# A transformer block on one core: where the reciprocals, the softmax sums and the input load stand in their slots

## The reference

```
x = x + layernorm(attention(layernorm(x)))
x = x + layernorm(ffn(layernorm(x)))

attention:  q, k, v = x @ w_q, x @ w_k, x @ w_v          # 16 heads of 64
            q = l2norm(q) * exp(scale);  k = l2norm(k)
            out = softmax(q @ k.T) @ v  ->  out @ w_out + b_out
ffn:        h = silu(x @ w1 * s1) * (x @ w2 * s2)        # 1024 wide
            h = gelu(h @ h1 * t1);  h = gelu(h @ h2 * t2);  h @ w3 * s3
```

## Time and profile before

| | us |
|---|---|
| median of 3 runs | 1771.52 (1770.67 to 1775.65) |
| the profiled execution | 1771.27 |
| its span, first to last instruction | 1769.4 |
| TensorE busy in the span | 1703.3 (96%) |
| VectorE busy | 1184.2 (67%) |
| ScalarE busy | 1010.7 (57%) |
| GpSimd busy | 461.4 (26%) |

### The profile page before, as it was taken

How to read it: one execution, slowest core, us unless ns; L and a number is a source line. 1 busy time by engine, 2 the same in 40 slices (tenths; PEclk the granted TensorE clock), 3 DMA queues, 4 the chain that set the end, 5 groups by cost and what they waited for, 6 DMA issues and landing times.

```text
span 1769.4 us, 24647 instructions
## 1 busy us (share of the span) xinstructions
PE 1703.3 (96%) x8584; PEld 1421.9 (80%) x8584; DVE 1184.2 (67%) x2033; ACT 1010.7 (57%) x1349; POOL 461.4 (26%) x557
## 2 busy tenths in 40 slices
PE   5999999999999999999999987999999999999998
PEld 4788888788888888888888775788888888888887
DVE  5777877877877877877877876635454545445454
ACT  4877778778778777777778765223223231323231
POOL 3533533533533533533633321000000000000000
PEclk9999999999999999999999999999999999999999
DMA  4545555456455456455455653300000000000000
GB/s 130 131 116 127 123 126 139 108 126 143 103 132 138 104 130 150 105 126 123 101 117 131 149 153 100 116 2 4 22 24 1 24 1 25 0 25 1 24 1 24
DMA packets 73473, 151.44 MB, mean 86 GB/s; under 512 B 27904, under 2 KB 28288, under 8 KB 73344
## 3 DMA queue, kind: packets, MB, share of 16 engines
q1 hardware_dynamic: 65712, 122.87, 29.2%
q10 hardware_dynamic: 6624, 23.21, 4.5%
q0 software_dynamic: 1008, 3.67, 0.5%
HBM read 56.91 MB, written 20.19 MB: 44 GB/s over the span
## 4 chain that ended last, share of the span: by engine, by line
PE 76%; DVE 8%; DMA 6%; issue 5%; ACT 3%; SPq 2%; POOL 1%; DVEq 0%; ACTq 0%; POOLq 0%
PE bank L1061 15%; PE pair L1139 13%; PE pair L1140 13%; PE bank L1003 10%; PE pair L1044 4%; PE pair L1045 4%; PE bank L1075 4%; PE pair L1130 3%; PE pair L1131 3%; DVE Pl L714 3%; PE bank L1030 2%; DMA Dp<-work 2%; PE bank L1168 2%; PE bank L1169 2%; DMA work<-rows 1%
## 5 line engine op out<-in xcount | busy, mean ns | idle before, releaser
L1139 PE MATMUL pair<-hh,f 128*128 128x512 f32 x1024 | 400.7, 391 | 2.6 <-DVE hl L832 2.2
L1140 PE MATMUL pair<-hl,f 128*128 128x512 f32 x1024 | 399.5, 390 | 0.0
L1061 PE MATMUL bank<-Ph,V 128*128 128x512 f32 x1024 | 367.3, 399 | 20.9 <-DVE Pl L714 19.1
L501 ACT ACTIVATE P<-pair,sh 128x1024 f32<-128x1024 f32 x256 | 286.3, 1118 | 159.8 <-PE pair L1045 136.3
L714 DVE TENSOR_TENSOR Pl<-P,Ph 128x1024 fp32r<-128x1024 f32 x256 | 315.4, 1232 | 0.3
L1003 PE MATMUL bank<-w,xh 128*128 128x256 f32 (+1 forms) x1024 | 285.3, 341 | 6.1 <-DVE turned L708 2.8
L549 ACT ACTIVATE hr<-pair,ct 128x512 f32<-128x512 f32 x128 | 88.3, 690 | 355.0 <-PE pair L1140 355.0
L506 ACT ACTIVATE Ph<-P 128x1024 fp32r<-128x1024 f32 x256 | 271.9, 1062 | 8.1
L1061 PEld LDWEIGHTS bank<-Ph,V 128*128 128x128 f32 x1024 | 192.9, 188 | 83.8 <-issue 38.9
L1139 PEld LDWEIGHTS pair<-hh,f 128*128 128x128 f32 x1024 | 192.8, 188 | 46.6 <-DVE hl L832 5.9
L1140 PEld LDWEIGHTS pair<-hl,f 128*128 128x128 f32 x1024 | 192.8, 188 | 39.9
(11 more groups left out here) (104 smaller groups left out, 2660.3 us busy)
## 6 DMA issues: line engine op xcount, KB each, us to landing
stack<-turned SPq DMA_DIRECT2D x128, 384.0 KB, 4.0
stack<-turned SPq DMA_DIRECT2D x128, 256.0 KB, 4.7
work<-rows SPq DMA_DIRECT2D x128, 128.0 KB, 2.9
f<-raw ACTq DMA_DIRECT2D x22, 512.0 KB, 4.9
raw<-in_h ACTq DMA_DIRECT2D x16, 512.0 KB, 4.0
xt<-in_x SPq DMA_DIRECT2D x8, 512.0 KB, 8.2
xr<-in_x SPq DMA_DIRECT2D x8, 512.0 KB, 4.6
x<-xr SPq DMA_DIRECT2D x8, 512.0 KB, 5.7
```

Of the source, the lines that this page charges most:

```text
L501: e.activation(M.P[:, i % 2, :], M.SB[i % 2][:, :], ACT.Exp, bias=M.sh[:, h:h + 1]).then_inc(S["exp"])
L1061: d = e.matmul(M.OB[:, :], v, p[:, u % 3, j * 512:(j + 1) * 512], start=jt == 0 and m == 0, stop=jt == 3 and m == 2)
L1139: e.matmul(ps, w, M.hh[src][:, k, :].bitcast(to), start=k == 0, stop=False)
L1140: d = e.matmul(ps, w, M.hl[src][:, k, :].bitcast(to), start=False, stop=k == KH - 1)
```

## The change

Three steps move. Nothing is added or taken away.

- On VectorE `invert` goes from behind `Pl` and the low part of the output to behind the value splits and the scalings of its slot (slots 3, 7, 11, ...).
- On SyncE the copy of the odd head of the pair that is turned in a slot with `i % 8 = 0` goes from the next slot to the one after it, where it stands behind `take_sums`. For the pairs of `i % 8 = 5` it stays in the next slot, where it was behind `take_sums` already.
- `load_x` of batch `b + 1` stood in slot 0 of batch `b`, three slots ahead of its first reader. Now that of batch 1 stands in slot 3 of batch 0 (the slot of the first reader), and that of batch `b + 2` in slot 27 of batch `b`, eight slots ahead.

```
@@ -316,16 +316,19 @@
             spread_rec(i // 4 - 2)
         if pair_of(i) is not None:
             stack(pair_of(i), 0)
-        if i and pair_of(i - 1) is not None:
-            stack(pair_of(i - 1), 1)
+        late = 2 if i % 8 == 2 else 1
+        if i >= late and i % 8 in (2, 6) and pair_of(i - late) is not None:
+            stack(pair_of(i - late), 1)
         if i % 4 == 3 and 0 <= i // 4 - 1 < NP:
             store_rec(i // 4 - 1)
...
-        if b + 1 < B and i32_ == 0:
-            load_x(b + 1)
+        if i == 3:
+            load_x(1)
+        if b + 2 < B and i32_ == 27:
+            load_x(b + 2)
         if live and i32_ == 28:
             load_xr(b)
@@ -890,8 +893,6 @@
             split_wo(i - 5 if i < 7 else i - 10)
         if i % 4 == 2 and 0 <= n - 3 < NP:
             o_low(n - 3)
-        if i % 4 == 3 and 0 <= n - 2 < NP:
-            invert(n - 2)
         if early and 0 <= n - 3 < NP:
             normal(n - 3)
@@ -916,6 +917,8 @@
             head_scale(u)
         if i % 4 == 1 and not early and 0 <= n - 3 < NP:
             normal(n - 3)
+        if i % 4 == 3 and 0 <= n - 2 < NP:
+            invert(n - 2)
         if quad_of(i) is not None:
             add_part(quad_of(i), 0)
             add_part(quad_of(i), 1)
```

## The result

The changed kernel takes 1765.49 us, the median of 13 runs (1760.99 to 1769.89), beside 1773.97 us for the kernel before in as many runs. The ratio is 0.9956 (95% interval 0.9945 to 0.9967): faster by 0.44%. Its profiled execution took 1763.06 us, 8.2 less than that of before, and its span is 1761.2 us against 1769.4.

What follows compares the result with a forecast made beforehand. TensorE was taken to set the pace in the attention part. Terms 5.0 + 0.9 + 2.5 - 1.0 - 1.2 - 1.0 = 5.2 us less than 1771.27, written as 1766 us; range 1760.5 to 1774.

Steps and rivals of the forecast that it cites:

- The six stops of slot 5: Slot 5 of batches 1 to 6: TensorE's six stops for `Pl` go, 5.0 us gained, bounds 3.5 and 5.0.
- the stack stops: TensorE's two stops at score products for late `stack` copies: half goes, 0.9 us gained, bounds 0 and 1.8.
- Batch 7: Slot 19: sums leave ahead of the odd copies, TensorE's stop goes, 2.5 us gained, bounds 1.2 and 3.0.
- Slots 27 to 29, with the load: Late reciprocal and load delay the broadcasts; TensorE stops 0.2 us in six batches, 1.2 us lost, bounds 0 and 12.
- the second rival: Slot 29, batches 0 to 5: broadcasts land behind the load, kernel slower, 1776.9 or 1780 us; chance 0.10 for over 1773.
- Slots 11 to 13: Late reciprocal delays the broadcasts to slot 13's products: 0.2 us in five batches, 1.0 us lost, bounds 0 and 7.4.
- Batch 0: Load for batch 1 is issued up to 2.6 us later: 1.0 us lost, bounds 0 and 2.6.
- The odd copies: Issued later by about one sum's issue, 1.69 us: cost nothing; otherwise ScalarE would wait for `stack` in slot 5.

Runs made afterwards that it cites:

- p_sums_load: Kernel before with the sums ahead of the odd copies and the load moved, the reciprocal left early: 1754.00 us, ratio 0.9884 to the kernel before.
- The repetition: The changed kernel as it is, timed and profiled once more against the kernel before: 1763.53 us, ratio 0.9946.
- the second profile: Profile of the changed kernel run once more, nothing altered; timed against the kernel before: 1763.53 us, ratio 0.9946.
- its repetition: The kernel before with sums first and load moved, reciprocal early, run once more: 1755.43 us, ratio 0.9895 to the kernel before.

## Why the prediction was right, step by step

The forecast was 1766 and the median came out at 1765.49, but that they meet within a microsecond is in part luck. The forecast starts from three runs of the kernel before, with a median of 1771.52, and its 13 runs have 1773.97. What the sum foretold is the gain: 5.2 us, where the medians are 8.5 apart and the profiled executions 8.2; 0.3%, where the ratio gives 0.44. The sum was right to about 3 us, and its largest terms were too small, on both sides.

**The six stops of slot 5, the stack stops.** Forecast 5.0 and 0.9, bounds up to 6.8. Slots 4 to 8 gained 7.7 us, 9.98 to 2.25. For the stops of `Pl` the mechanism is right: the sums leave within a microsecond of `Ev`, the wait is gone, `Pl` follows, and the stop of 1.14 us in the earlier trace rows has no counterpart. The step that failed was to take the column "idle before" as the price of a stop. TensorE of the kernel before, ahead of batch 1:

```profile
184.57 0.39 PE L1044 MATMUL pair<-stack 128*128 128x512 f32 x1
184.80 0.40 PE L1045 MATMUL pair<-stack 128*128 128x512 f32 x1
185.78 0.47 PE L1061 MATMUL bank<-Ph,V 128*128 128x512 f32 x1 [0.58 <-DVE Pl L714]
186.09 0.39 PE L1061 MATMUL bank<-Pl,V 128*128 128x512 f32 x1
...
188.60 0.39 PE L1044 MATMUL pair<-stack 128*128 128x512 f32 x1
188.83 0.39 PE L1045 MATMUL pair<-stack 128*128 128x512 f32 x1
189.33 0.47 PE L1061 MATMUL bank<-Ph,V 128*128 128x512 f32 x1
189.64 0.40 PE L1061 MATMUL bank<-Pl,V 128*128 128x512 f32 x1
```

Matmuls overlap: a row lasts 0.39 us, but the next starts 0.23 us later (184.57, 184.80). With a stop, the next starts 0.98 later and the one behind it 0.31 later, so 0.75 and 0.08 are lost where 0.58 is shown. The second place shows no idle time at all, and loses 0.27 and 0.08. Both together are 1.18 us by these rows, and these four slots took 1.33 more than in `p_sums_load`. I had counted 0.58. A stop costs about 0.25 us more than is shown, and a short one is not shown.

The 0.9 us for the `stack` stops did not come. Before, TensorE stopped twice for a `stack` copy in batches 1 to 6, 1.8 us in sum; after, three times, 2.6 us, the third being that of 0.97 us at 492.18:

```profile
200.86 0.47 PE L1047 MATMUL pair<-stack 128*128 128x512 f32 x1 [0.99 <-issue]
...
590.76 0.47 PE L1047 MATMUL pair<-stack 128*128 128x512 f32 x1 [0.67 <-issue]
```

The repetition has two of them, 1.7 us, so by what these profiles can tell the change neither cures nor makes them. The two shown are most of what is left in slots 4 to 8 (1.21 us in batch 1 and 0.42 in batch 4 of the 2.2).

**Batch 7.** Forecast 2.5, bounds 1.2 and 3.0; the column says 5.6 (4.2 to -1.4). The stop of 2.49 us went, as said, and slots 20 to 24 take 2.5 us less. Behind them stops came and went. TensorE, before and then after:

```profile
1053.61 1.10 PE L1030 MATMUL bank<-ident,qk 128*128 128x128 f32 x8 [2.62 <-DVE flag L784]
```

```profile
1039.87 0.47 PE L1064 MATMUL bank<-Ph,V 128*128 128x512 f32 x1 [1.74 <-DVE Pl L717]
...
1047.81 1.09 PE L1033 MATMUL bank<-ident,qk 128*128 128x128 f32 x8 [1.11 <-DVE flag L787]
```

The stop for `flag` is 1.5 us shorter, but one of 1.74 us for `Pl` is new. The same instructions differ by up to 4.8 us in this column from one profile to another, and I can't assign the remainder.

**Slots 27 to 29, with the load.** Forecast 1.2 lost, bounds 0 and 12; measured 4.7 (4.6 more than before), and 5.9 in the second profile. This is the term that failed most. I had the broadcasts land 6.0 to 6.4 us after the reciprocal and VectorE lose 1.0 to 1.4; it is 6.7 in batch 3, and the waits ahead of the products are 2.76, 0.96, 1.22, 2.32, 1.77 and 1.54 us, 1.76 on the mean. And the slack behind them was 0.9, not 1.3: the losses follow the waits less 0.93 us. The two errors, about half a microsecond and 0.4, together turn my 0.2 per batch into 0.8. That the loss is there at all, and that the load stands behind half of it, is what the second rival said; its price was between my term and its.

**Slots 11 to 13.** Forecast 1.0 lost, bounds 0 and 7.4. VectorE waits 0.10 us ahead of the products of slot 13 in batch 1 and not at all in the other batches, and slots 12 to 16 take 0.05 to 0.08 us longer in five batches, about 0.3 in sum. The broadcasts were in time; no load stands in their way there.

**Slot 5, which I had left out.** The sum has no term for the products of slot 5, which hang on the late reciprocal of slot 3 as those of slot 29 hang on that of slot 27. The waits before them, up to 0.92 us, say that it should; what they cost is at most what the `stack` stops leave of the 2.2 us in slots 4 to 8.

**Batch 0.** Forecast 1.0 lost, bounds 0 and 2.6. The wait for the input grew from 0.62 us to 1.38:

```profile
53.10 0.43 DVE L650 BATCH_NORM_STATS2 st<-xt 128x6 f32<-128x256 f32 x1 [1.38 <-DMA xt<-in_x]
```

The exponential of slot 8 comes 0.6 us later. Another 1.4 us are lost in slots 8 to 12, where the forecast had nothing; they go with a fall of the clock, as told below.

**The odd copies.** Nothing, as forecast: ScalarE doesn't wait for `stack` in slot 5. It does so four times elsewhere (slots 0, 8, 16 and 24 of batch 7), 5.1 us in sum, and did so four times with 5.1 us before (slot 8 of batch 0, and slots 8, 16 and 24 of batch 7).

By the columns, then: 7.7 and 5.6 gained, 4.6 lost at slot 29, 0.6 and 1.4 in batch 0, 0.3 in slots 11 to 13, and 1.4 gained behind the attention, which the edits don't touch: 7.8 us, beside 8.2 of the spans. The total was near because gains and losses were both taken too small: 8.4 us gained where the columns have 13.3, of which some in batch 7 may be chance, and 3.2 lost where they have 6.9.

## What to carry to other kernels

When several edits aim at the same wait, make each alone before all together: here any one removed the stops, and the third one only brought its cost. A step that waits without holding up the bottleneck is not worth moving for its wait, and what hangs behind it (here a round trip through memory, 6.7 us long) counts from where it stands, not from where its input lands. Price a stop of TensorE by the starts of the matmuls around it, not by its idle time.

## What the runs showed of the hardware

**A stretch at a lower clock.** TensorE between 60 and 82 us of the span (length of the stretch, busy time, matmuls recorded, granted clock, DMA share, GB/s), before and after:

```profile
60.00:82.00 22.00, 19.71 (x94) 1.00 0.66 157
```

```profile
60.00:82.00 22.00, 19.98 (x84) 0.92 0.62 148
```

The mean granted clock of this stretch is 0.92 of full speed (2.4 GHz) in seven of thirteen profiles and 1.00 in the others. Each of the three steps occurs on both sides (`p_sums_load` has 1.00, its repetition 0.92), so it is not an effect of the change. Finer stretches show what the mean hides. In the kernel after:

```profile
67.14 0.47 PE L1047 MATMUL pair<-stack 128*128 128x512 f32 x1 [2.02 <-DMA stack<-turned]
```

```profile
69.00:70.00 1.00, 1.00 (x4) 0.50 0.80 179
```

TensorE has stood still for 2.02 us up to 67.14, and about a microsecond later its granted clock is at 0.50, the lower of its two levels (1.2 GHz). In the microsecond from 72 it is at 1.00 again, after at least 3 us at the lower level, in which TensorE was busy throughout. All thirteen profiles have this stop, with 1.98 to 2.29 us; the fall follows in seven, and the length of the stop doesn't decide it: the longest, 2.29 us before, has none. All seven lose 0.7 to 1.6 us in slots 8 to 12 of batch 0 against `p_sums_load`, and none of the others more than 0.04. Why the fall comes in one execution and not in the next stays open.

**A stop that no edit moved.** In ten of the thirteen profiles TensorE stops about 1.0 us (0.75 to 1.20), one to three times, at a score product of slots 12 to 16 whose `stack` copy isn't there, most often in batch 3 (0.97 us at 492.18 in the kernel after, 1.00 at 492.79 before). It costs about 1.2 us each time. I made no experiment on it, and its cause stays open.

**Behind the attention.** The spans differ by up to 6.6 us behind the last exponential, in code that no edit touches. A part of it is again the clock: between 40 and 50 us behind that exponential the mean granted clock is 0.83 in six profiles and 1.00 in the seven others. The six take 1.1 to 5.9 us longer there than `p_sums_load`, the others between 0.7 less and 1.9 more. What sets it, and the remainder, stay open.
